# Last group's feed-forward as a tail of two units (three tiles and one), its late features by TensorE: a six-layer windowed-attention kernel

## The reference

```
def shift_tokens(t):
    a, s = jnp.split(t, 2, -1)
    s = jnp.pad(s, ((0, 0), (1, 0), (0, 0)))[:, :-1]
    return jnp.concatenate([a, s], -1)

def ffn_layer(x, g, bln, W1, b1, W2, b2):          # 128 -> 2 x 341 -> 128
    xn = (x - mean) / sqrt(var + 1e-05) * g + bln
    a, gate = jnp.split(xn @ W1 + b1, 2, -1)
    return a * gelu(gate) @ W2 + b2

for i in range(6):
    x = attn_layer(shift_tokens(x), ...) + x
    x = ffn_layer(shift_tokens(x), ...) + x
out = x_mid + layernorm(x)                          # x_mid: the input of the six layers, before its layernorm
```

## Time and profile before

| | |
|---|---|
| median of 3 runs | 1619.39 us (1618.85 to 1620.7) |
| profiled execution, its own time | 1619.38 us |
| its span | 1617.6 us |
| TensorE (matmul) busy | 1544.3 us, 95% |
| VectorE / ScalarE / GpSimd busy | 1234.8 / 1232.5 / 1222.1 us, 76% each |
| mean granted clock of TensorE | 0.987 of 2.4 GHz |

### The profile page before, as it was taken

How to read it: one execution, slowest core, us unless ns; L and a number is a source line. 1 busy time by engine, 2 the same in 40 slices (tenths; PEclk the granted TensorE clock), 3 DMA queues, 4 the chain that set the end, 5 groups by cost and what they waited for, 6 DMA issues and landing times.

```text
span 1617.6 us, 69676 instructions
## 1 busy us (share of the span) xinstructions
PE 1544.3 (95%) x30224; PEld 907.8 (56%) x30224; DVE 1234.8 (76%) x1693; ACT 1232.5 (76%) x2368; POOL 1222.1 (76%) x1051
## 2 busy tenths in 40 slices
PE   7879999999999999999999999999999999999995
PEld 6745556555555555555556555555565565555553
DVE  5488878778778778777877778778778788787873
ACT  4347787787787787887887887887887887887871
POOL 6169888777787778778777787787787787787861
PEclk9989999999999999999999999999999999999998
DMA  5000000100000100000100000100000000000000
GB/s 193 28 2 27 10 7 5 61 7 6 22 6 7 35 29 10 18 7 9 36 28 10 9 16 10 33 31 9 9 16 9 7 5 9 7 18 9 7 12 27
DMA packets 24545, 32.60 MB, mean 20 GB/s; under 512 B 2372, under 2 KB 21424, under 8 KB 23344
## 3 DMA queue, kind: packets, MB, share of 16 engines
q1 hardware_dynamic: 24240, 28.15, 5.4%
HBM read 20.80 MB, written 1.05 MB: 14 GB/s over the span
## 4 chain that ended last, share of the span: by engine, by line
PE 75%; ACT 7%; issue 5%; DVE 3%; POOL 1%; DMA 0%; ACTq 0%; SPq 0%; POOLq 0%; DVEq 0%
PE ring L274 20%; PE psq L254 18%; PE ring L262 9%; PE ring L308 8%; PE pss L292 7%; PE ring L325 4%; PE ring L318 4%; PE pss L283 2%; DVE qb L927 2%; ACT L1126 2%; ACT sq L1096 1%; ACT uT L1126 1%; ACT pr L1100 1%; ACT kT L1107 1%; PE ring L649 1%
## 5 line engine op out<-in xcount | busy, mean ns | idle before, releaser
L254 PE MATMUL psq<-wqk,x0S 128*128 128x512 f32 x768 | 379.4, 617 | 4.0 <-issue 3.1
L274 PE MATMUL ring<-mh,x0S 128*32 128x512 f32 x3072 | 369.6, 598 | 7.4 <-ACT uT L1126 7.4
L1305 POOL TENSOR_TENSOR qa<-qa,qb 128x1024 f32<-128x1024 f32 x96 | 228.9, 2384 | 63.0 <-DVE qb L848 62.9
L1361 POOL TENSOR_TENSOR pr<-pr,rden 128x1024 f32<-128x1024 f32 x96 | 183.9, 1915 | 88.3 <-DVE rden L824 88.0
L1357 POOL TENSOR_TENSOR qa<-qa,qb 128x1024 f32<-128x1024 f32 x96 | 226.7, 2361 | 0.4 <-DVE qb L927 0.3
L254 PEld LDWEIGHTS psq<-wqk,x0S 128*128 128x128 f32 x768 | 135.8, 192 | 130.0 <-issue 120.8
L308 PEld LDWEIGHTS ring<-u,pT 128*32 128x32 f32 x6144 | 172.9, 111 | 61.4 <-issue 61.4
L904 DVE TENSOR_TENSOR qa<-psq,tab 128x1024 f32<-128x1024 f32 x96 | 117.5, 1224 | 105.5 <-PE psq L254 105.5
L308 PE MATMUL ring<-u,pT 128*32 128x128 f32 x6144 | 187.0, 274 | 3.2 <-ACT pT L1228 3.2
L1323 POOL TENSOR_TENSOR qa<-qa,rn 128x1024 f32<-128x1024 f32 x96 | 182.7, 1903 | 7.5
L274 PEld LDWEIGHTS ring<-mh,x0S 128*32 128x32 f32 x3072 | 80.0, 109 | 190.5 <-issue 172.6
(11 more groups left out here) (174 smaller groups left out, 2819.8 us busy)
## 6 DMA issues: line engine op xcount, KB each, us to landing
wqk<-in_wqk SPq DMA_DIRECT2D x6, 1024.0 KB, 4.9
mvT<-in_mvT SPq DMA_DIRECT2D x6, 512.0 KB, 5.6
wo<-in_wo SPq DMA_DIRECT2D x6, 512.0 KB, 8.7
xf<-x SPq DMA_DIRECT2D x24, 128.0 KB
xf<-x SPq DMA_DIRECT2D x24, 127.0 KB
rope<-in_rope SPq DMA_DIRECT2D x1, 2048.0 KB, 10.0
w<-in_w SPq DMA_DIRECT2D x6, 341.0 KB, 3.8
xmid<-in_x SPq DMA_DIRECT2D x4, 256.0 KB, 4.0
```

The costliest lines, as they stand in the source:

```text
L254: return mm(psq[:, 512 * (n % 2):512 * (n % 2) + 512], x0S[:, tile * P:tile * P + P], wqk[:, l % 2, 512 * n:512 * n + 512], start=True, st ...
L274: last = mm(bank[WIN * g:WIN * g + WIN, :], x0S[:, tile * P + WIN * w:tile * P + WIN * w + WIN], mh[:, l % 2, g, :, :].rearrange("p j n -> ...
L1305: g_.tensor_tensor(qa[:, t % 2, 0:1024], qa[:, t % 2, 0:1024], qb[:, 0:1024], ALU.add).then_inc(sum_q, 1)
L1361: g_.tensor_tensor(p4[t % 2], p4[t % 2], rden[:, :].unsqueeze(1).unsqueeze(3).broadcast_to([P, 2, HEADS, WIN]), ALU.mult).then_inc(p_ready, 1)
```

## The change

The loop no longer makes group 23: `group_at` ends at group 22. Behind the loop each engine gets a tail that makes the four tiles as two units, one of three tiles and one of one tile, each with its own instructions, semaphores and output transfer. The late features come from TensorE: a shift matrix `late` (made by GpSimd in the loop, in the memory of `mh` that the last layer no longer reads) moves the rows of `x1[:, 1]` down by one partition in two matmuls for each unit, and ScalarE copies own and late features into `xf`. The three transfers into `xf` are gone for this group. Statistics, roots, normalisation, transposes, hidden and narrow products, sum and last normalisation are the same computation as before, on three tiles and on one. In the diff, ring banks of the tail are named TL (late rows), TF (transposes), TG/TA (hidden), TZ (narrow); `tail_turn`, `tail_narrow`, `tail_gate`, `tail_turned`, `tail_gelu` are left out, being the loop's items with the unit's columns.

```diff
+TAIL = [(0, 3), (3, 1)]
...
-    return n // QUAD if n >= 0 and n % QUAD == 0 and n // QUAD < ALLG else -1
+    return n // QUAD if n >= 0 and n % QUAD == 0 and n // QUAD < ALLG - 1 else -1
...
+        late = mh[:, 0, 0:2].rearrange("p g j n -> p (g j n)")[:, 0:2 * P]
...
+            def late_rows(v):
+
+                k0, n = TAIL[v]
+                bank, m = take("TL", v)
+                ybank, use = place["Y", STEPS - QUAD + k0 + n - 1]
+                pe.wait_ge(freed[ybank], use + 1)
+                wait(pe, t_late, 2)
+                wait(pe, freed[bank], m)
+                for d in range(2):
+                    tiles = slice(1 + TILES - QUAD + k0 - d, 1 + TILES - QUAD + k0 - d + n)
+                    last = mm(ring[bank][:, 0:n * HD], late[:, d * P:d * P + P], x1[:, 1, tiles, :].rearrange("p k n -> p (k n)"),
+                              start=(d == 0), stop=(d == 1))
+                last.then_inc(filled[bank], 1)
...
+            def tail_hidden(v, k, gate):
+
+                k0, n = TAIL[v]
+                bank, m = take(("TA%d", "TG%d")[gate] % k, v)
+                nbank, use = place["TF", v]
+                pe.wait_ge(freed[nbank], use + 1)
+                wait(pe, freed[bank], m)
+                h0, rows = HBLK[k]
+                col = h0 + gate * HID
+                mm(ring[bank][0:rows, 0:n * P], w1[:, col:col + rows], xnT[:, k0 * P:(k0 + n) * P],
+                   start=True, stop=True).then_inc(filled[bank], 1)
...
+            late_rows(0)
+            late_rows(1)
+            for v in range(len(TAIL)):
+                tail_turn(v)
+                for k in range(3):
+                    tail_hidden(v, k, 1)
+                    tail_hidden(v, k, 0)
+                if v > 0:
+                    tail_narrow(v - 1)
+            tail_narrow(len(TAIL) - 1)
...
+            def tail_stats(u):
+
+                k0, n = TAIL[u]
+                bank, m = place["TL", u]
+                dve.wait_ge(freed[bank], m + 1)
+                for k in range(k0, k0 + n):
+                    last = v.bn_stats(bst[:, k, :], xf[:, :, k, :])
+                last.then_inc(t_bst, 1)
+                dve.wait_ge(t_bst, u + 1)
+                for k in range(k0, k0 + n):
+                    last = v.bn_aggr(mv[:, k, :], bst[:, k, :])
+                last.then_inc(t_mv, 1)
...
+            def tail_sum(u):
+
+                k0, n = TAIL[u]
+                first = TILES - QUAD + k0
+                bank, m = place["TZ", u]
+                dve.wait_ge(filled[bank], m + 1)
+                v.tensor_tensor(x0T[:, first:first + n, :].rearrange("p k (a n) -> p k a n", a=2),
+                                 ring[bank][:, 0:n * P].rearrange("p (k a n) -> p k a n", k=n, a=2),
+                                 x1[:, :, 1 + first:1 + first + n, :].rearrange("p a k n -> p k a n"), ALU.add).then_inc(t_x0, 1)
...
+            def tail_out(u):
+
+                k0, n = TAIL[u]
+                first = TILES - QUAD + k0
+                dve.wait_ge(t_frs, u + 1)
+                for k in range(k0, k0 + n):
+                    t = TILES - QUAD + k
+                    last = v.tensor_scalar(x0T[:, t, :], x0T[:, t, :], fmv[:, GROUPS - 1, k, 0:1], frstd[:, GROUPS - 1, k:k + 1],
+                                            ALU.subtract, ALU.mult)
+                last.then_inc(t_fn, 1)
+                dve.wait_ge(t_fn, u + 1)
+                part = xmid[:, first:first + n, :]
+                v.tensor_tensor(part, x0T[:, first:first + n, :], part, ALU.add).then_inc(t_out, 1)
+
+            for u in range(len(TAIL)):
+                tail_stats(u)
+            for u in range(len(TAIL)):
+                for k in range(3):
+                    tail_gate(u, k)
+                if u > 0:
+                    tail_sum(u - 1)
+            tail_out(0)
+            tail_sum(len(TAIL) - 1)
+            tail_out(1)
...
+            for v, (k0, n) in enumerate(TAIL):
+                tiles = slice(1 + TILES - QUAD + k0, 1 + TILES - QUAD + k0 + n)
+                bank, m = place["TL", v]
+                act.wait_ge(filled[bank], m + 1)
+                cp(xf[:, 0, k0:k0 + n, :], x1[:, 0, tiles, :])
+                cp(xf[:, 1, k0:k0 + n, :], ring[bank][:, 0:n * HD].rearrange("p (k n) -> p k n", n=HD)).then_inc(freed[bank], 1)
+
+            def tail_hat(v):
+
+                k0, n = TAIL[v]
+                act.wait_ge(t_nmr, v + 1)
+                abank, m = place["A2", ALLG - 2]
+                act.wait_ge(filled[abank], m + 1)
+                for k in range(k0, k0 + n):
+                    last = nc.scalar.activation(xh[:, k * P:k * P + P].rearrange("p (a n) -> p a n", a=2), xf[:, :, k, :],
+                                                ACT.Identity, bias=nmr[:, k:k + 1], scale=rstd[:, k:k + 1])
+                last.then_inc(t_xh, 1)
+
...
+            for v in range(len(TAIL)):
+                tail_hat(v)
+            tail_turned(0)
+            for v in range(len(TAIL)):
+                if v > 0:
+                    tail_turned(v)
+                for k in range(3):
+                    tail_gelu(v, k)
...
+                if s == STEPS - QUAD:
+                    bank, n = place["Y", STEPS - TILES - 1]
+                    pool.wait_ge(filled[bank], n + 1)
+                    g_.memset(late, 0.0).then_inc(t_late, 1)
+                    pool.wait_ge(t_late, 1)
+                    g_.tensor_copy(late[:, 1:1 + P], ident[:, :]).then_inc(t_late, 1)
...
+            for v, (k0, n) in enumerate(TAIL):
+                part = slice(k0, k0 + n)
+                pool.wait_ge(t_mv, v + 1)
+                roots(mv[:, part, :], n, vare[:, part], rstd[:, part], mrs[:, part], nmr[:, part], t_rs, 3 * v).then_inc(t_nmr, 1)
+            for v, (k0, n) in enumerate(TAIL):
+                part = slice(k0, k0 + n)
+                pool.wait_ge(t_fmv, v + 1)
+                g_.tensor_tensor(fvare[:, GROUPS - 1, part], fmv[:, GROUPS - 1, part, 1:2].rearrange("p k o -> p (k o)"), eps[:, 0:n],
+                                 ALU.add).then_inc(t_fv, 1)
+                pool.wait_ge(t_fv, v + 1)
...
-            sp.wait_ge(s_out, 16 * GROUPS)
+            for v, (k0, n) in enumerate(TAIL):
+                sp.wait_ge(t_out, v + 1)
+                tiles = slice(TILES - QUAD + k0, TILES - QUAD + k0 + n)
+                sp.dma_start(out_v[:, tiles, :], xmid[:, tiles, :]).then_inc(s_out, 16)
+            sp.wait_ge(s_out, 16 * (GROUPS - 1 + len(TAIL)))
```

More of the change, by code:

```diff
@@ L223, in build @@
             sem(n) for n in ("f_stats", "f_var", "f_rstd", "f_norm", "f_out", "s_out"))
+        t_late, t_bst, t_mv, t_rs, t_nmr, t_xh, t_x0, t_fbst, t_fmv, t_fv, t_frs, t_fn, t_out = (
+            sem(n) for n in ("t_late", "t_bst", "t_mv", "t_rs", "t_nmr", "t_xh", "t_x0", "t_fbst", "t_fmv", "t_fv",
+                             "t_frs", "t_fn", "t_out"))
         NCONST, NTABLES = 3, 6
@@ new lines, in tail_turn @@
+            def tail_turn(v):
+                k0, n = TAIL[v]
+                bank, m = take("TF", v)
+                pe.wait_ge(t_xh, v + 1)
+                wait(pe, freed[bank], m)
+                for k in range(n):
+                    last = tr(ring[bank][:, k * P:k * P + P], xh[:, (k0 + k) * P:(k0 + k) * P + P], ident[:, :])
+                last.then_inc(filled[bank], 1)
+            def tail_hidden(v, k, gate):
[3 more added lines that the diff above has]
+                pe.wait_ge(freed[nbank], use + 1)
+                wait(pe, freed[bank], m)
+                h0, rows = HBLK[k]
+                col = h0 + gate * HID
+                mm(ring[bank][0:rows, 0:n * P], w1[:, col:col + rows], xnT[:, k0 * P:(k0 + n) * P],
+                   start=True, stop=True).then_inc(filled[bank], 1)
@@ new lines, in tail_narrow @@
+            def tail_narrow(v):
+                k0, n = TAIL[v]
+                bank, m = take("TZ", v)
+                for k in range(3):
+                    abank, use = place["TA%d" % k, v]
+                    pe.wait_ge(freed[abank], use + 1)
+                wait(pe, freed[bank], m)
+                for k in range(n):
+                    for j, (h0, rows) in enumerate(HBLK):
+                        rows += j == 2
+                        last = mm(ring[bank][:, k * P:k * P + P], uT[0:rows, j, (k0 + k) * P:(k0 + k) * P + P], w2[0:rows, j, :],
+                                  start=(j == 0), stop=(j == 2))
+                last.then_inc(filled[bank], 1)
@@ new lines, in tail_gate @@
+            def tail_gate(u, k):
+                k0, n = TAIL[u]
+                cols = slice(k0 * P, (k0 + n) * P)
+                bank, m = place["TA%d" % k, u]
+                dve.wait_ge(filled[bank], m + 1)
+                gbank, use = place["TG%d" % k, u]
+                dve.wait_ge(freed[gbank], use + 1)
+                rows = HBLK[k][1]
+                v.scalar_tensor_tensor(uT[0:rows, k, cols], ring[bank][0:rows, 0:n * P], par[0:rows, LAYERS - 1, 2 + k:3 + k],
```

(46 more changed lines are left out.)

2 lines of the change are left out of this document (added).

## The result

The median of the change is 1623.13 us (22 runs, 1617.81 to 1627.0) against 1620.62 us for the kernel before, measured beside it (22 runs, 1617.46 to 1625.92): ratio 1.0015, 95% interval [1.0008, 1.0022]. That is 2.5 us slower, clear of zero; the ratio lies inside the 0.2% that was named as the edge, while its interval reaches to 0.22%. The forecast was 1622.8 us, 0.21% slower, with about even chances for the two sides of that edge.

What follows compares the result with a forecast made beforehand. TensorE bounds the loop (busy 1544 of 1617.6 us), but this change acts in the last 35 us' chain of waits. Terms -0.1, -0.65, +1.7, 0, +2.4, 0 sum to +3.4 on 1619.39: 1622.8 us, range 1620.3 to 1624.7.

Steps and rivals of the forecast that it cites:

- the edge: Whole kernel: about 0.2% (3.2 us) tells a measurement from no change; chances slower 0.50, same 0.47, faster 0.03.
- Step 1: After the loop: without the copy, group 22's last gate ends about 1585.4, its narrow product 1588.35, xf whole about 1590.5.
- Step 2: VectorE's queue: tail statistics stand behind group 22's 5.2 us of work, starting 1593.6 instead of 1591.67; 1.9 us lost.
- Step 3: From tail statistics to first hidden product: starts 1600.3 against 1600.37 today, -0.1 us, containing the two steps before it.
- Steps 4 and 7: Tail's hidden and narrow products: 8.6 us at high clock against 9.25, gain 0.65; low clock after idle time loses 2.4.
- Step 5: The end: two VectorE round trips to GpSimd one after the other, 6.95 us against 5.24, loss 1.7.
- Step 6: Last output transfer shrinks from 256 to 64 KB: no change taken, bounds 1.7 us less to 0.4 more.
- Step 8: GpSimd's fill and copy for the shift matrix in the loop: under 0.72 us each, hidden by slack, costing nothing.
- A: Tail's wide products: transposes help the clock return, so nearly all run at the high level; 1620.4 us, no change; chance 0.13.
- B: Tail's wide products: half clock through all (+3.9 instead of +2.4), plus 0.5 us ring bank waits; 1624.8 us; chance 0.07.
- C: Tail's start: VectorE reads xf at 1590.5, all 3.1 us earlier, no clock loss; 1617.3, or 1615.6 with short transfer; chance 0.03.

Runs made afterwards that it cites:

- t5: The change with its late features taken back to the three transfers of before, units kept; median 1623.35 us, ratio 1.0007 to the kernel before.
- t3: The change with the tail's two statistics moved up in VectorE's list, right behind group 22's aggregation; median 1619.18 us, ratio 0.9996 to the kernel before.
- t2: The change plus nine idle products on TensorE between late rows and the tail's transposes, holding the clock; median 1619.91 us, ratio 0.9998 to the kernel before.
- t1: The changed kernel measured once more, unaltered; median 1621.89 us, ratio 1.0013 to the kernel before.
- t4: The change with the second unit's sum, statistics and aggregation ahead of the first unit's normalisation in VectorE's list; 1620.48 us, ratio 1.0005 to the kernel before.
- t7: The change with statistics early, second sum first and six idle products for the clock; median 1616.17 us, ratio 0.9971 to the kernel before.
- t11: The kernel before with only group 22's last gate moved ahead of the last group's statistics in VectorE's list; median 1621.66 us, ratio 1.0003.
- t8: The kernel before with ten idle products ahead of group 22's narrow product, holding the clock; median 1620.41 us, ratio 0.9991.
- t10: The t7 kernel measured once more, unaltered; median 1615.54 us, ratio 0.9962 to the kernel before.

## Why the prediction was right, step by step

*The time.* Right, within the interval, and for the reasons given: queue, clock, order at the end. That the median came within 0.3 us of the forecast is in part luck. The forecast stood on a base of 1619.39 us, and the kernel before measured 1620.62 beside the change, 1.2 us more; the difference came out 0.9 us less than forecast. The sum was made for the tail, +3.4 us; the two medians say +2.5 and +2.1 (intervals 1.3 to 3.6 and 0.6 to 3.6), the tails of the two profiles +2.1 and +0.8 against the one profile of the kernel before. The profiled execution's +3.5 us matches the forecast only by chance, since 1.4 us of it are in the loop. Inside the sum, terms that were too high and one that was too low partly cancel, as the steps show.

*Step 1, the copy goes.* Forecast: group 22's last gate ends 2.3 us after the last attention sum ends, then 2.96 us. Measured: 2.4 us (1584.43 to 1586.80) and 2.96. xf is whole 7.2 us after the last attention sum starts, forecast 7.7.

*Step 2, the queue.* Forecast 10.8 us from the start of the last attention sum to the first statistics, measured 10.84. t5 showed that the copy's length has no part in it and t3 that the queue has.

*Step 3, the first wide product.* Forecast level with before (0.1 us less), measured 0.9 us less: 16.68 us after the last attention sum against 17.60. This is the term that was mis-sized: the roots. From the end of the aggregation to the first activation three columns take 1.84 us (1596.00 to 1597.84), not 2.4, and the roots of one column 1.4 us, not 2.1. Both had been taken from the 2.5 us of the kernel before, and that stretch holds one small product of 0.66 us beside an add of VectorE, which takes 0.24 us in the change. Before:

```profile
1594.64 0.69 DVE L950 TENSOR_TENSOR xmid<-x0T,xmid 128x512 f32<-128x512 f32 x1
1594.76 0.66 POOL L1344 TENSOR_SCALAR nmr<-mrs 128x4 f32<-128x4 f32 x1
```

The change, roots of the one-tile unit:

```profile
1597.57 0.24 POOL L1449 TENSOR_SCALAR nmr<-mrs 128x3 f32<-128x3 f32 x1
1597.78 0.19 POOL L1443 TENSOR_TENSOR vare<-mv,eps 128x1 f32<-128x1 f32 x1
...
1598.04 0.58 POOL L1445 TENSOR_TENSOR rstd<-vare,neg_half 128x1 f32<-128x1 f32 x1
1598.70 0.19 POOL L1447 TENSOR_TENSOR mrs<-mv,rstd 128x1 f32<-128x1 f32 x1
1598.98 0.23 POOL L1449 TENSOR_SCALAR nmr<-mrs 128x1 f32<-128x1 f32 x1
```

The power of one column is 0.58 us, under the 0.73 that the rows for two and four columns suggest. So the evacuation at 1600.10 waits for the transposes, slow at the low clock, and not, as was forecast, for the other unit's activation. In t2, where the transposes are fast, it does wait for it.

*Steps 4 and 7, products and clock.* Forecast 8.6 + 2.4 = 11.0 us from the first wide product to the sum, measured 11.57 in the first profile. With the clock held (t2) this stretch is 8.81 us, near the 8.6. Five profiles with the tail's two units and a free clock (change, t1, t3, t4, t5) have 5.52 to 6.89 us for the wide products, 6.29 in the mean, against 4.14 with the clock held: 2.15 us in the mean, near the 2.4 taken from the earlier trace rows. The 5.5 to 6.5 us that the prediction named for them held in three of the five (5.52, 5.97, 6.25) and not in the change's own profile (6.89) or in t3 (6.80).

*Step 5, the end.* Forecast 6.95 us, measured 6.69; t4 confirmed that the order alone makes the second trip.

*Step 6, the last transfer.* Taken as unchanged. The DMA issues of the change:

```profile
out<-xmid SPq DMA_DIRECT2D x3, 256.0 KB, 2.3
...
out<-xmid SPq DMA_DIRECT2D x1, 64.0 KB, 1.5
```

It lands 0.8 us sooner, and the span ends 2.02 us after the last write in place of 2.74. The 64 KB load of the opening, 2.7 us, was a poor neighbour; why it took longer than this write no run shows. By the fit on the Trainium skill's page "DMA: Bandwidth & Descriptors" ("Anatomy of one DMA"), made on transfers that GpSimd issues, the piece would have saved an estimated 0.45 us of 2.6. Here SyncE issues it, and it saved 0.8 of 2.3 (0.6 to 0.8 in the other runs with two units), so size mattered somewhat more than by that fit. So the tail's 3.4 forecast became 2.1: 0.8 less by step 3, 0.7 less by step 6, 0.3 less by step 5, and 0.6 more by steps 4 and 7.

*Step 8, fill and copy.* Right: 0.31 and 0.29 us, hidden.

*The rivals.* A did not come true: the three transposes brought no clock back, which returned at 1606.4. B's wait for banks was refuted by t2, whose wide products take 4.14 us where 4 was the sum without any wait; its half clock through all the wide products did not come either. C's mechanism was real, its reach was not: with VectorE out of the way the first wide product came 2.4 us earlier (t3), and the kernel was level with before, not faster; t7, with all three repairs, got there. The forecast did not see that C's, the clock's and the end's losses could all be taken away by three small edits.

## What to carry to other kernels

Before a wait is taken away, read what the waiting engine has queued behind it: here 8.5 us of transfer gave way to 5.2 us of another group's work, and the kernel became faster than before only once two blocks of VectorE's list were moved and the clock was held. A round trip to another engine should be given work of the next unit, in the list and not only in the plan: the split into units lost 1.6 us at its end by one call in the wrong place, and is worth 2.4 us when it is right (with the clock held). An estimate of a small operation's time should be taken from a row in which the other engine was as busy as it will be: the 2.5 us for the roots held 0.4 us of a meeting with VectorE's add that the change no longer has. At a program's end TensorE's idle time should be put where little work follows it, or filled.

## What the runs showed of the hardware

The clock fell 2 us after TensorE's last work in the change and 4 us after it in the kernel before, and the work that followed ran at the low level for 5.6 us from the first wide product; the time of the same twelve instructions varied from 5.52 to 6.89 us in five profiles, three of which (change, t1, t5) agree in the rest of the tail within 0.1 us. A stretch that follows idle time has to be read from more than one profile.

A small operation of GpSimd (128x3 or 128x4) takes 0.19 to 0.24 us alone and 0.66 us beside a VectorE add of two tensors in the chip's memory. It was so in the kernel before as well: `nmr` (L1344) took 0.66 us beside VectorE's L950, and 0.24 in the change, where VectorE was idle. Its end goes by the add's end: in t11 the product began 0.42 us into the add and took 0.33 us, and in before, t3, t8, t10 and t11 the small operation ended 0.05 to 0.09 us after the add did. Beside VectorE's sum (L805 in t11), one of whose inputs lies in PSUM, `nmr` took 0.23 us. The Trainium skill names such a contention in "GPSIMD Engine Reference", Specifications: GpSimd's interfaces to that memory are shared with VectorE, with contention beside VectorE instructions that have two inputs there. The traces agree, with 0.42 to 0.47 us more for one such meeting.

What stays open is the scatter of the whole. The last attention sum started between 1579.9 and 1589.4 us in thirteen profiles of kernels whose loops are the same. The mean granted clock between 60 and 110 us was between 0.69 and 0.83 in them, and the two highest (0.83 and 0.80) belong to two early loop ends, but a third early one had 0.73. No run here isolated it.
